# Gate, up and down products of a feed-forward layer as seven block products over pairs of token tiles

## The reference

```python
# layer 0: a base projection with one LoRA adapter for each sequence, then a gated feed-forward
c  = x @ W.T + b + 2.0 * (x @ A[slot]) @ B[slot]
h  = silu(c @ W_gate.T) * (c @ W_up.T)            # 512 -> 1376
x2 = x + h @ W_down.T                             # 1376 -> 512
# layer 1: a projection with top-2 LoRA experts, then another projection with top-2 LoRA experts
out = x2 + layer1(x2)
```

## Time and profile before

| what | value |
|---|---|
| median of three runs | 1107.45 us (1104.37 to 1108.0) |
| the profiled execution's own time | 1105.8 us |
| its span, first to last instruction | 1104.1 us |
| PE busy | 1083.9 us, 98% |
| DVE, ACT, POOL busy | 33%, 22%, 9% |
| mean granted TensorE clock | 0.998 |
| moved by DMA | 80.64 MB |

### The profile page before, as it was taken

The page is one execution under the profiler, slowest core; times in us unless marked ns, Lnnn a source line. Parts: engine busy times, 40 slices in busy tenths (PEclk is TensorE's granted clock), DMA queues, the critical chain, the costliest instruction groups (busy, mean ns, idle before and its releaser), DMA issues.

```text
span 1104.1 us, 12516 instructions
## 1 busy us (share of the span) xinstructions
PE 1083.9 (98%) x5168; PEld 900.2 (82%) x5168; DVE 359.2 (33%) x659; ACT 242.7 (22%) x433; POOL 95.9 (9%) x103
## 2 busy tenths in 40 slices
PE   6899999999999999999999999999999999999998
PEld 5788888888888888887888888888788687888887
DVE  3553522221212212212222221221221147665663
ACT  3543431111211111211111121121111132222310
POOL 3544436000000000000000000000000000000000
PEclk9999999999999999999999999999999999999999
...
GB/s 225 234 220 221 227 140 111 1 17 98 1 1 115 1 0 115 1 1 96 20 1 5 111 1 1 115 1 1 153 1 106 11 31 47 105 77 108 103 45 61
DMA packets 49065, 80.64 MB, mean 73 GB/s; under 512 B 5636, under 2 KB 15884, under 8 KB 48752
## 3 DMA queue, kind: packets, MB, share of 16 engines
...
...
## 4 chain that ended last, share of the span: by engine, by line
PE 96%; DMA 1%; DVE 1%; ACT 1%; issue 0%; POOL 0%; SPq 0%; POOLq 0%; DVEq 0%; ACTq 0%
PE ring L835 52%; PE acc L835 43%; PE ring L947 1%; DMA c_scratch<-c_out 1%; PE ring L855 0%; DMA slot_i<-in_slots 0%; DMA ab<-in_ab_table,row_i 0%; DVE act_lo L622 0%; ACT act_hi L474 0%; DVE hg_lo L742 0%; DVE a_lo L629 0%; ACT a_hi L482 0%; DVE res L755 0%; DVE hg L734 0%; SPq L326 0%
## 5 line engine op out<-in xcount | busy, mean ns | idle before, releaser
L835 PE MATMUL ring<-act_hi,gate_up 128*128 128x512 f32 (+1 forms) x1408 | 447.2, 390 | 0.0
L835 PEld LDWEIGHTS ring<-act_hi,gate_up 128*128 128x128 f32 (+1 forms) x1408 | 261.0, 185 | 58.4
L835 PE MATMUL ring<-act_lo,gate_up 128*128 128x512 f32 (+1 forms) x704 | 274.2, 389 | 0.0
L655 DVE TENSOR_TENSOR s_buf<-s_buf,ring 128x512 f32<-128x512 f32 (+1 forms) x88 | 60.5, 687 | 490.7 <-PE ring L835 490.7
L835 PEld LDWEIGHTS ring<-act_lo,gate_up 128*128 128x128 f32 (+1 forms) x704 | 130.5, 185 | 29.5
L835 PE MATMUL acc<-h_hi,down_hi 128*128 128x512 f32 (+1 forms) x352 | 137.1, 389 | 0.0
L835 PE MATMUL acc<-h_lo,down_hi 128*128 128x512 f32 (+1 forms) x352 | 137.0, 389 | 0.0
L835 PE MATMUL acc<-h_hi,down_lo 128*128 128x512 f32 (+1 forms) x352 | 136.9, 389 | 0.0
L508 ACT ACTIVATE s_buf<-ring 128x512 f32<-128x512 f32 (+1 forms) x88 | 52.6, 598 | 329.8 <-PE ring L835 329.8
L516 ACT ACTIVATE h_hi<-s_buf 128x512 fp32r<-128x512 f32 (+1 forms) x88 | 55.6, 632 | 257.2 <-DVE s_buf L655 257.2
L622 DVE TENSOR_TENSOR act_lo<-raw,act_hi 128x512 fp32r<-128x512 f32 x96 | 72.2, 789 | 38.9 <-ACT act_hi L474 38.9
(11 more groups left out here) (123 smaller groups left out, 1118.7 us busy)
## 6 DMA issues: line engine op xcount, KB each, us to landing
raw<-in_x SPq DMA_DIRECT2D x32, 256.0 KB, 4.6
c_scratch<-c_out SPq DMA_DIRECT2D x32, 256.0 KB, 2.5
raw<-c_scratch SPq DMA_DIRECT2D x32, 256.0 KB, 3.6
res<-in_x SPq DMA_DIRECT2D x32, 256.0 KB, 4.9
x_scratch<-res SPq DMA_DIRECT2D x32, 256.0 KB, 2.0
raw<-x_scratch SPq DMA_DIRECT2D x32, 256.0 KB, 4.1
out<-res SPq DMA_DIRECT2D x32, 256.0 KB, 2.0
stage<-in_w_gate SPq DMA_DIRECT2D x10, 256.0 KB, 4.0
```

What stands on the lines that cost most here:

```text
L655: e.tensor_tensor(s_buf[s][0:f, :], s_buf[s][0:f, :], ring_bank("up", t, j)[0:f, :], ALU.mult).then_inc(dve_freed, 1)
L835: return e.matmul(out_ap, lhs, rhs, start=start, stop=stop, skip_group_check=True)
```

## The change

Stage F now works on pairs of token tiles, s = 0 to 3 (NS = 4). With the weight matrix cut into 2 x 2 blocks and the pair of tiles with their two feature halves also as 2 x 2 blocks, the eight block products become seven (numbered 1 to 7), each of a sum of weight blocks with a sum of activation blocks. In the gate and up product, the gate weights are the upper blocks (a11, a12) and the up weights the lower (a21, a22); for each of the now 11 full chunks j (the last is padded with zeros to 128 rows) each block product is 2 x 3 = 6 matmuls. In the down product chunks are taken in five pairs p, and the eleventh alone without the scheme (`down_single`).

Around it:

- **Weight sums.** In stage C, POOL makes four sums of gate and up blocks for each pair of chunks jp (`gate_up_sums`), ACT and DVE or POOL split seven blocks per jp (`gate_up_hi`, `gate_up_lo`; 42 steps), and SP stores each to DRAM (`store_gate_up`, up to 512 KB each). The 42 steps are spread over the 24 feature chunks of tiles 0 to 5 (`g_due`), with four buffers `gt`. The sums and splits of the down weights follow in the same way inside stage F of s = 0 (22 steps, `d_due`, two buffers `dt_`, `store_down`).
- **Streamed weights.** Weights no longer stay in SBUF. Each block product of each chunk reads one 256 KB slot of a ring of 12 (`load_slot`, `take_slot`), loaded again for each s. `slot_order` sets the order: 114 slots for one s, 77 of the gate and up product, 35 of the down product, and 2 of `down_single`.
- **Activation sums.** c of two tiles is read back (`load_c`), POOL makes four sums for each half (`c_sum`), and ACT and DVE split seven operands for each (`cop_split`, `cop_rest`, 14 for each s). For s + 1 this is done in the down part of s, behind the steps that `COP_BEHIND` names. In the down part POOL makes four sums for each of the five pairs of h (`t3_t1`, `t2`, `t4`), and ACT and DVE split 35 operands (`op_split`, `op_rest`), into four buffers (N_OP = 4).
- **Joining.** The results are made out of partial sums by DVE (`sum_u2`, `sum_u3`, `sum_c21`, `sum_c22`, `sum_c12`, two products for each j, and 14 such steps in the down part), with POOL adding residuals.
- **The weight products of stage L** come after the last slot, no longer ahead of the last gate and up product.

The core of the diff:

```diff
+    G_ORDER = [1, 2, 4, 5, 6, 7, 3]
+    G_POOL = (5, 6, 7)
+    g_steps = [(jp, i) for jp in range(NP + 1) for i in G_ORDER]
+    g_turn = {st: n for n, st in enumerate(g_steps)}
+    g_points = 4 * (NT - 2)
+    def g_due(t, m):
+        q = KC * t + m
+        return range(len(g_steps) * q // g_points, len(g_steps) * (q + 1) // g_points) if q < g_points else range(0)
...
+    D_ORDER = [1, 6, 2, 7, 5, 4, 3]
+    slot_order = []
+    for j in range(NF):
+        slot_order += [("g", j, 1), ("g", j, 6)] + ([("g", j - 1, 3)] if j else [])
+        slot_order += [("g", j, 4), ("g", j, 2), ("g", j, 7), ("g", j, 5)]
+    for i in D_ORDER:
+        if i == 3:
+            slot_order += [("s", 1, 0), ("s", 0, 0)]
+        slot_order += [("d", i, p) for p in range(NP)]
+        if i == 1:
+            slot_order += [("g", NF - 1, 3)]
+    N_SLOT = len(slot_order)
...
+    op_order = [(i, p) for i in D_ORDER for p in range(NP)]
...
+    COP_BEHIND = {9 + (n * 25) // len(cop_order): n for n in range(len(cop_order))}
...
+        def store_gate_up(n):
+            jp, i = g_steps[n]
+            e.wait_ge(*g_lo_count(n))
+            c = chunks_of(jp)
+            e.dma_start(wgu_dram[2 * jp:2 * jp + c, i].rearrange("j p f -> p j f"),
+                        plain(gt[n % 4][:, 0:c, :, :, :]).rearrange("p j h q c -> p j (h q c)"),
+                        ).then_inc(gt_stored[n % 4], DMA)
...
+        def load_slot(n):
+            s, pos = divmod(n, N_SLOT)
+            kind, a, b = slot_order[pos]
+            if n >= N_W:
...
+                    e.wait_ge(gt_stored[st % 4], DMA * (st // 4 + 1))
+                src = wgu_dram[a, b]
+            elif kind == "d":
+                if s == 0:
+                    st = d_turn[b // 2, a]
+                    e.wait_ge(dt_stored[st % 2], DMA * (st // 2 + 1))
+                src = wd_dram[b, a]
+            else:
+                if s == 0:
+                    e.wait_ge(ws_stored, DMA)
+                src = ws_dram[a]
+            e.dma_start(plain(wring[n % N_W][:, :]), src).then_inc(w_in[n % N_W], DMA)
...
+            if s == 0:
+                for j in range(NF - 1):
+                    if pos == slot_at["g", j, 5]:
+                        for n in d_due(j):
+                            store_down(n)
+                        for g in (2, 3):
+                            if d_turn[g - 2, 3] in d_due(j):
...
+                e.dma_start(b2_raw[:, :], b2t).then_inc(b2_in, DMA)
+                load_unit(0)
...
+        def t2(s, p):
+            e.wait_ge(t1_done, NP * s + p + 1)
+            e.wait_ge(op_lo_done, op_n(s, 1, p) + 1)
+            e.tensor_tensor(h11[p][:, :], h22[p][:, :], h12[p][:, :], ALU.subtract).then_inc(t2_done, 1)
+        def t4(s, p):
+            e.wait_ge(t2_done, NP * s + p + 1)
+            e.wait_ge(op_lo_done, op_n(s, 2, p) + 1)
+            e.tensor_tensor(h21[p][:, :], h21[p][:, :], h11[p][:, :], ALU.subtract).then_inc(t4_done, 1)
...
+                    t3_t1(s, j // 2 - 1)
+            for p in range(NP):
+                t2(s, p)
+            if s + 1 < NS:
+                for i in (3, 1, 2):
+                    c_sum(s + 1, 0, i)
+            for p in range(NP):
+                t4(s, p)
+            if s + 1 < NS:
+                c_sum(s + 1, 0, 4)
+            for mp in range(2):
+                u2_residual(s, mp)
+            if s + 1 < NS:
+                for i in (3, 1):
+                    c_sum(s + 1, 1, i)
+            for mp in range(2):
+                v1_residual(s, mp)
+            if s + 1 < NS:
+                for i in (2, 4):
+                    c_sum(s + 1, 1, i)
+            for mp in range(2):
+                out22(s, mp)
 
         e.wait_ge(ra1_in, DMA)
...
+        def op_rest(s, i, p):
+            n = op_n(s, i, p)
+            e.wait_ge(op_hi_done, n + 1)
+            e.tensor_tensor(op_lo[n % N_OP][:, :], op_source[i][p][:, :], plain(op_hi[n % N_OP][:, :]),
+                            ALU.subtract).then_inc(op_lo_done, 1)
...
+        def sum_u2(s, j):
+            b = j % 2
+            e.wait_ge(pe_slot, slot_n(s, "g", j, 6) + 1)
+            e.wait_ge(p1s_done, NF * s + j + 1)
+            if s > 0 and j < 2:
+                e.wait_ge(x2_stored["c12", b], DMA * s)
+            e.tensor_tensor(u2[b][:, :], bank_y[b][:, :], p1s[b][:, :], ALU.add).then_inc(u2_done, 1)
...
+        def product_1(s, j):
+            b, n = j % 2, NF * s + j
+            e.wait_ge(silu1_done, n + 1)
+            e.wait_ge(gc21_done, n + 1)
+            if j < 2 and s > 0:
+                e.wait_ge(op_lo_done, len(op_order) * s)
+            dst = v1[0] if j == NF - 1 else (h11, h21)[j % 2][j // 2]
+            e.tensor_tensor(dst[:, :], p1s[b][:, :], v1[b][:, :], ALU.mult).then_inc(h1_done, 1)
...
+                if j >= 2 and j % 2 == 0 and j // 2 - 1 < N_OP:
+                    op_rest(s, 1, j // 2 - 1)
+            sum_c22(s, NF - 1)
+            product_1(s, NF - 1)
+            for n in range(N_OP, len(op_order)):
+                op_rest(s, *op_order[n])
+                if n == 8:
+                    sum_c12(s, NF - 1)
+                    product_2(s, NF - 1)
+                if n == 10:
+                    h10_rest(s, 0)
+                if n == 12:
+                    h10_rest(s, 1)
+                if n == 13:
+                    down_u2(s, 0)
+                    down_u2(s, 1)
+                if n == 23:
+                    down_u3(s, 0)
+                    down_u3(s, 1)
+                if n == 28:
+                    down_z22(s, 0)
+                    down_z22(s, 1)
+                if s + 1 < NS and n in COP_BEHIND:
+                    cop_rest(s + 1, *cop_order[COP_BEHIND[n]])
...
+        def take_slot(n):
+            e.wait_ge(w_in[n % N_W], DMA * (n // N_W + 1))
+            return wring[n % N_W]
+        def gate_up(s, j, i):
+            b, n = j % 2, NF * s + j
...
+                    e.wait_ge(c_closed, nth(NT - 1))
+                else:
+                    e.wait_ge(*ring_freed("h", NT - 1, 0))
+            if i == 1 and j >= 2:
+                e.wait_ge(silu1_done, n - 1)
+            if i == 1 and j < 2 and s > 0:
...
+            if i == 7:
+                e.wait_ge(u2_done, n + 1)
+            if i == 3:
+                e.wait_ge(gc22_done, n + 1)
...
-                    done.then_inc(pe_acc, 1)
-                elif m == KC - 1:
-                    done.then_inc(pe_down, 1)
+                e.wait_ge(cop_lo_done, cop_n(s, 1, i))
+            wt = take_slot(slot_n(s, "g", j, i))
+            for q in range(2):
+                done = mm3(bank[:, :], wt[:, q * P:(q + 1) * P], wt[:, (2 + q) * P:(3 + q) * P],
+                           cop_hi[i][:, q, :], cop_lo[i][:, q, :], q == 0 and i in (1, 6, 4, 5), q == 1)
+            done.then_inc(pe_slot, 1)
...
 
-        for t in range(NT):
-            for j in range(NF):
-                if t == NT - 1 and j == NF - 1:
-                    for i in range(KC + 1):
-                        weight_product(i)
-                gate_up(t, j)
-                if j > 0:
-                    down(t, j - 1)
-            if t == NT - 1:
-                route_x(0)
-            down(t, NF - 1)
-
+        for s in range(NS):
+            for kind, n, i in slot_order:
+                if kind == "g":
+                    gate_up(s, n, i)
+                elif kind == "d":
+                    down(s, n, i)
+                else:
+                    down_single(s, n)
+        for i in range(KC + 1):
+            weight_product(i)
```

More of the change, by code:

```diff
@@ new lines, in cop_split @@
+        def cop_split(s, q, i):
+            n = 2 * s + q
+            if (s, q, i) == (0, 0, C_ORDER[0]):
+                for r in range(4):
+                    e.wait_ge(gt_stored[r], DMA * len([k for k in range(len(g_steps)) if k % 4 == r]))
+            if s > 0 and (q, i) == (0, C_ORDER[0]):
+                e.wait_ge(pe_slot, slot_n(s - 1, "g", NF - 1, 3) + 1)
+            if i in (1, 2, 3):
+                e.wait_ge(cst_in[{1: 0, 2: 2, 3: 3}[i]], DMA * (n + 1))
+            else:
+                e.wait_ge({4: c_t4_done, 5: c_t1_done, 6: c_t2_done, 7: c_t3_done}[i], n + 1)
+            e.activation(cop_hi[i][:, q, :], cop_source[i][:, :], ACT.Copy).then_inc(cop_hi_done, 1)
@@ L526, in weight_product, with split_unit @@
                 e.activation(ra2[:, :], bank[:, 0:LH], ACT.Copy).then_inc(act_freed, 1)
+        def split_unit(t):
+            s = l_slot(t)
+            for k in range(KC):
+                e.wait_ge(raw_in[s][k], DMA * (t // 3 + 1))
+                if k == 0 and t >= 3:
+                    e.wait_ge(pe_acc, nth(NT + t - 3))
+                e.activation(act_hi[s][:, k, :], raw[s][:, k, :], ACT.Copy).then_inc(l_hi, 1)
         def route_x(t):
@@ L858, in lora_in @@
         def lora_in(t):
-            s = slot(t)
+            s = t % 2
             bank = take_ring("h", t, 0)
@@ new lines, in down_single @@
+        def down_single(s, half):
```

(12 more changed lines are left out.)

1052 lines of the change are left out of this document (729 added, 323 removed).

## The result

The changed kernel takes 1115.5 us (median of 8 runs, 1112.9 to 1119.2), the kernel before 1107.5 us in the same session. The ratio is 1.0083, with a 95% interval of 1.0064 to 1.0103: **0.8% slower**, where 1094 us, 1.2% faster, was forecast. The time lies inside the range of 1055 to 1148 us, but on the other side of the kernel before.

A forecast was written before the change was run, and what follows sets the result against it. PE was taken as the bound, by its number of matmuls. From 1105.8 us, -87.2 (PE) + 13 + 5 (stage C, step to F) + 12 (s = 0) + 32 (down parts) + 3 + 4 (joints, end) + 6 (clock) gave 1094 us, range 1055 to 1148.

The forecast's parts named there:

- The gain on PE: Four pairs of tiles in stage F save 384 matmuls at 0.2271 us each: 87.2 us less.
- The down parts: Stage F's down parts: DVE and POOL hinder each other, +10 us per s < 3, +2 for s = 3, together +32.
- the lock: Down parts: DVE instructions with two SBUF inputs and POOL's SBUF reads exclude one another; at least +6, up to +16 per s.
- The gate part of s = 0: Stage F, s = 0: down-weight splits and their stores delay the steps PE waits for; +12 us, bounds 4 and 25.
- Stage C and the step to F: Stage C: added stores on DMA, +13 us; step to stage F: late operands of c's second half, +5.
- The clock: PE's granted clock falls after waits, some four as long as stage L's one of 2 us; +6 us, bounds 0 and 20.
- The joints: Between two s, DVE's last steps stand before the next products 1 and 7; +3 us for three joints, bounds 0 and 9.
- the end: Last down part, s = 3: DVE and POOL +2 us, layer 1's loads put ahead of the slots +3.
- The rivals: Covers hold better (0.20), 1053 to 1070 us; DMA is the bound (0.20), 1142; clock drops in down parts (0.15), 1136.
- the DMA rival: DMA bounds: stage C at 331 GB/s with gaps +35, stores in s = 0 +25; 1142 us, chance 0.20.
- The forecast's own case: Whole kernel: the summed terms give 1094 us, 1074 to 1115 with their smaller bounds; chance 0.45.

The follow-up runs named there:

- The run with fills: Changed kernel with POOL's sums of the down parts replaced by two memsets each, which read nothing; sums not computed: 1072.4 us, ratio 0.9697 to the kernel before.
- the run with filled waits: Changed kernel with 44 useless matmuls added on PE before three waits, around the start of stage F and s = 0: 1114.6 us, ratio 1.0069 to the kernel before.

## Why the prediction was wrong

- **The gain on PE: right.** 384 matmuls fewer; the gate parts of s > 0, forecast at 104.6 us, took 104.3 to 104.4.
- **The down parts: the right mechanism, put too low, and this is the step that failed.** The text named the lock, bounded it by +6 and +16 for each s and chose +10, "since some of the 16 PSUM sums and DVE's waits for a free buffer lie beside POOL". It was +14.4. The +10 means that 5.5 of POOL's 31 us are covered and DVE never stands (39 + 31 - 5.5 = 64.5). DVE was busy for 40.1 us with the fills and for 60.2 with the sums, so some 20 of the 31 us were put on it and 11 were covered, more than was forecast. What failed is that DVE's waits were to lie beside POOL. In s = 1 DVE stood for 8.9 us, of them 5.65 for a free operand buffer at the end, 2.13 for c and 0.70 for ACT, and POOL stood in all three. The sum had nothing for such time: 40.1 + 20 + 8.9 = 69.0 us. That this is near the bound of strict alternation (39 + 31 = 70) is chance.

  The three parts are 13 us over the forecast. The run with fills shows that the loss hangs on POOL's reads; that the place of the waits made the size is read from this one trace, and no run moved them alone. The rule of the Trainium skill (SBUF — State Buffer, Who interferes with whom), that a VectorE instruction with two SBUF inputs and a GpSimd instruction that reads SBUF keep one another out for a whole instruction, agrees with the trace (0.69 against 1.75 us); the error is in the sum made from it.
- **The gate part of s = 0: +21.3 for +12.** The forecast priced a split's wait for a store at +4 in two j, and put the clock in a term of its own. PE's waits for u there are five, 10.8 us together, and the clock fell to 0.92 around them. Moving the steps ahead of silu1 gave back 11 us, so the mechanism was the named one for half of the loss; the other half stays open.
- **Stage C and the step to F: +24.3 for +18.** The rate was as taken (357 to 369 GB/s at a share near 1.0, against 350). The bytes are worth 14 us with most of them taken away, close to the +13. The rest, 10 us for the +5, is on the way of the last chunk (3.5 us for c_out, 1.5 of issue) and in waits for a_lo, 4.5 us even with fewer stores, which the sum had at nothing. DMA stood at 0.76 from 28 to 56 us, so the bytes did not fill the stretch evenly; that the blocks were not ready by then is my reading.
- **The clock: +6 for a granted clock that gave away some 22 us of PE's full-speed time** (0.04 x 182 + 0.08 x 126 + 0.02 x 138 + 0.03 x 60). But the run with filled waits gave back under 4 of the 10 us in s = 0, and a down part took as long at 0.95 as at 1.00. The granted clock overstates the loss where PE waits anyway. How much the clock cost in all was not measured; it is no term of the table, since it lies inside its rows.
- **The joints: about 0 for +3; the end: +5.8 for +5.** PE is idle 0.8 us in the gate part of s = 1. In s = 3 it waits 4.0 us for the weight ring behind layer 1's loads; with the loads spread out and no POOL sums, nothing is lost there.
- **The rivals.** None of them happened as a whole. The ring was waited for once, 4 us in s = 3, so loads did not bound the down parts; the clock of the down parts stayed at 0.97 or more. But the part of the DMA rival that had s = 0 at +25 came near its 21.3, and what half of that is stays open. The forecast's own case came true at the upper end of its 1074 to 1115 us. That span was a judgement: the terms' own bounds add up to 1041 and 1187 us. Three terms stood above their forecast at once (+13.2 in the down parts, +9.3 in the gate part of s = 0, +6.3 in stage C), which is what made a gain of 1.2% a loss of 0.8%; that the joints and the clock came in lower took back up to 9. I had let the terms vary apart from one another. That they go together, since each hangs on queues in strict order, is my reading and was not tested.
